# The selective scan's sum over 16 states as accumulating fp32 transposes, and projection weights held for two directions at a time

## The reference

```python
def step(h, inp):
    u_l, d_l, B_l, C_l = inp
    dA = jnp.exp(d_l[..., None] * A)
    dBu = d_l[..., None] * B_l[:, :, None, :] * u_l[..., None]
    h = dA * h + dBu
    y = jnp.sum(h * C_l[:, :, None, :], axis=-1)
    return (h, y)
```

## Time and profile before

| | us |
|---|---|
| runs of the kernel (3) | 27558.77 to 27562.47, median 27561.47 |
| span of the profiled execution | 27568.2 |
| one block of the scan in the steady part (b = 10, first sample) | 68.57 |
| the scan's stage per sample, first scan to last | 2193.7 |
| granted TensorE clock, mean over the span | 0.946 |

### The profile page before, as it was taken

The page is one execution under the profiler, slowest core; times in us unless marked ns, Lnnn a source line. Parts: engine busy times, 40 slices in busy tenths (PEclk is TensorE's granted clock), DMA queues, the critical chain, the costliest instruction groups (busy, mean ns, idle before and its releaser), DMA issues. The chain is left out here.

```text
span 27568.2 us, 304787 instructions
## 1 busy us (share of the span) xinstructions
PE 25221.1 (91%) x87136; PEld 12623.8 (46%) x87136; DVE 23267.7 (84%) x22864; ACT 21119.6 (77%) x39912; POOL 21256.1 (77%) x9545
## 2 busy tenths in 40 slices
PE   8999879998799987999879998799987999879998
PEld 3455434554345543455434554345543455434554
DVE  6799867998679986799867998679986799867998
ACT  4799747997479974799747997479974799747997
POOL 3799737997379973799737997379973799737997
PEclk8999989999899998999989999899998999989999
DMA  0122101221012210122101221012210122101221
GB/s 8 46 63 63 45 10 46 63 63 45 9 46 63 63 45 10 46 63 63 45 9 46 63 63 45 9 46 63 63 45 8 46 64 63 45 8 46 64 63 45
DMA packets 796847, 1243.41 MB, mean 45 GB/s; under 512 B 220801, under 2 KB 238081, under 8 KB 792065
## 3 DMA queue, kind: packets, MB, share of 16 engines
q1 hardware_dynamic: 795136, 1223.32, 15.1%
HBM read 1155.89 MB, written 67.11 MB: 44 GB/s over the span
## 5 line engine op out<-in xcount | busy, mean ns | idle before, releaser
L1590 PE MATMUL ps<-arena,ident 128*128 128x512 f32 x24576 | 11420.8, 596 | 2.8 <-DVE arena L1425 1.8
L1413 DVE TENSOR_TENSOR_SCAN arena<-arena,ps 128x512 f32<-128x512 f32 x7680 | 9263.5, 1264 | 102.1 <-ACT arena L1776 62.5
L1966 POOL TENSOR_TENSOR arena<-arena 128x1536 f32<-128x1536 f32 x1920 | 6631.5, 3459 | 72.8 <-ACT arena L1796 72.0
L1590 PEld LDWEIGHTS ps<-arena,ident 128*128 128x128 f32 x24576 | 4350.6, 190 | 4319.6 <-issue 4008.2
L1787 ACT ACTIVATE scaled<-arena,cols 128x384 f32<-128x384 f32 x10240 | 5807.7, 606 | 676.6 <-PE ps L1559 676.4
L1413 DVE TENSOR_TENSOR_SCAN arena<-ps,arena 128x512 f32<-128x512 f32 x4608 | 5583.2, 1264 | 74.7 <-ACT ps L1776 74.7
L1956 POOL TENSOR_TENSOR arena<-arena 128x1536 f32<-128x1536 f32 x1536 | 5306.2, 3463 | 321.9 <-DVE arena L1413 320.7
L1776 ACT ACTIVATE arena<-arena 128x512 f32<-128x512 f32 x7680 | 5240.7, 713 | 11.6 <-PE ps L1590 11.6
L1559 PEld LDWEIGHTS ps<-ident,scaled 128*128 128x128 f32 x30720 | 3524.8, 141 | 1982.0 <-issue 1113.1
L1559 PE MATMUL ps<-ident,scaled 128*128 128x128 f32 x30720 | 4182.0, 275 | 140.2 <-ACT scaled L1787 60.7
L1776 ACT ACTIVATE ps<-arena 128x512 f32<-128x512 f32 x4608 | 3125.0, 683 | 64.2 <-DVE arena L1413 25.1
(11 more groups left out here) (190 smaller groups left out, 33141.8 us busy)
## 6 DMA issues: line engine op xcount, KB each, us to landing
arena<-rows SPq DMA_DIRECT2D x3456, 256.0 KB, 3.2
spare<-rows SPq DMA_DIRECT2D x640, 256.0 KB, 3.3
arena<-x SPq DMA_DIRECT2D x16, 1536.0 KB, 13.4
x<-arena SPq DMA_DIRECT2D x16, 1536.0 KB, 10.7
arena<-x SPq DMA_DIRECT2D x64, 384.0 KB, 8.3
out<-arena SPq DMA_DIRECT2D x64, 384.0 KB, 3.0
rows<-xd SPq DMA_DIRECT2D x256, 64.0 KB, 2.6
arena<-L_conv_fc_w SPq DMA_DIRECT2D x16, 576.0 KB, 5.3
```

The costliest lines, as they stand in the source:

```text
L1413: nc.vector.tensor_tensor_scan(flip(states(b, n, t)), flip(decays), flip(adds), carry[:, k, N2 * n + t:N2 * n + t + 1], ALU.mult, ALU.add) ...
L1590: nc.tensor.matmul(m.ps[:, t, :], m.ident[:, :], states(b, n, t), start=False, stop=(n == SUMS[t][-1])).then_inc(at[Y_MM[t]], 1)
L1966: nc.gpsimd.tensor_tensor(out, out, each, ALU.mult).then_inc(at["hp_ready"], 1)
```

## The change

The 16 products of a tile are no longer added by a matmul with the identity as weights. Each is now the stationary operand of four 128 x 128 transposes that accumulate in bank t, so the bank holds the sum transposed, pixels on partitions. At the end of a block ACT copies the bank to an SBUF tile `y_turned` (`lift_y`), PE transposes that back into the same bank (`turn_y`, four transposes) and adds the old y or the skip product behind it in the same accumulation, and ACT copies the bank to y (`give_y`). `take_old` is gone; its product moved into `turn_y`. `lift_y` waits for the 16 sums and for the `turn_y` before (one `y_turned`), `turn_y` for its `lift_y`, `give_y` for its `turn_y`, and the first `add_up` of the next block for `give_y`. To make room for `y_turned`, the projection weights stand in two places instead of four; those of directions 2 and 3 are fetched by SP at blocks 8 and 16.

```diff
--- before.py
+++ after.py
@@ -1290,23 +1290,26 @@
 N4 = T // 128
 
 
+def rows_weights(xpw, a, k):
+
+    src = a["x_proj_w"][:, k, :].rearrange("(t p) c -> p t c", p=128)
+    return [(xpw[:, k % 2, :, 2 * NS * i:2 * NS * (i + 1)], src[:, :, DTR:]) for i in range(3)] + [
+        (xpw[:, k % 2, :, P:], src[:, :, 0:DTR])]
+
+
 def scan_weights(m, a):
 
     m.start(0)
-    xpw = m.take(K4, N2, P + DTR)
+    xpw = m.take(2 * N2, P + DTR).rearrange("p (k t) c -> p k t c", k=2)
     m.start(SLOTS)
     dtw = m.take(K4, D2)
     aneg = m.take(K4, N2, NS)
     dtb = m.take(K4, N2)
     dsk = m.take(K4, N2)
-    BC = 2 * NS
-    xw = a["x_proj_w"]
     loads = []
     for k in range(K4):
-        src = xw[:, k, :].rearrange("(t p) c -> p t c", p=128)
-        for i in range(3):
-            loads.append((xpw[:, k, :, BC * i:BC * (i + 1)], src[:, :, DTR:]))
-        loads.append((xpw[:, k, :, P:], src[:, :, 0:DTR]))
+        if k < 2:
+            loads += rows_weights(xpw, a, k)
         loads.append((dtw[P:P + DTR, k, :], a["dt_w"][:, k, :]))
         loads.append((aneg[:, k, :, :], a["A_logs"][k * D2:(k + 1) * D2, :].rearrange("(t p) n -> p t n", p=128)))
         loads.append((dtb[:, k, :], columns(a["dt_b"][k, :], 128)))
@@ -1314,7 +1317,7 @@
     return (xpw, dtw, aneg, dtb, dsk), loads
 
 
-def selective_scan(m, xc, y, weights, rows):
+def selective_scan(m, xc, y, weights, rows, a):
 
     nc = m.nc
     xpw, dtw, aneg, dtb, dsk = weights
@@ -1322,7 +1325,7 @@
     sp_l = m.take(T)
     sp_w = m.take(T)
     m.start(0)
-    m.take(K4, N2, P + DTR)
+    m.take(2 * N2, P + DTR)
     bbc = m.take(RB, T)
     cbc = [m.take(T) for _ in range(RC - 1)] + [m.spare]
     delta = m.take(2, N2, T)
@@ -1330,6 +1333,7 @@
     hs = m.take(HS, N2 * T)
     dbu = m.take(DB, N2 * T)
     turned = m.take(N4, D2)
+    y_turned = m.take(T)
     assert m.top <= 6 * SLOT, m.top
     scaled, xd, sp_e = m.scaled, m.xd, m.sp_e
     m.start(SLOTS)
@@ -1367,7 +1371,8 @@
     Y_MM = [f"y_mm_{t}" for t in range(N2)]
     names = ("filled", "ds_summed", "exped", "negated", "skip_out", "xd_mm", "hi_out", "xd_out", "mid_out", "sub_mm",
              "parts_out", "dl_mm", "sp_act", "sp_dve", "sp_pool", "kept", "turn_mm", "turn_out", "da_ready", "db_ready", "scanned",
-             "saved", "c_mm", "hc_ready", "hp_ready", "scaled_out", "back_mm", *B_IN, *C_IN, *Y_MM, "y_out")
+             "saved", "c_mm", "hc_ready", "hp_ready", "scaled_out", "back_mm", *B_IN, *C_IN, *Y_MM, "y_up", "y_turn", "y_back", "y_out",
+             "xpw_in")
 
     def nth(b, n, which):
 
@@ -1505,7 +1510,9 @@
                     return
                 if b and t == 0:
                     pe.wait_ge(at["turn_out"], (N4 + 1) * b)
-                ins = nc.tensor.matmul(shaped(b, m.ps[0:P + DTR, AH, :]), xpw[:, b // NT, t, :], block_of(b, xc, t),
+                if b >= 2 * NT and t == 0:
+                    pe.wait_ge(at["xpw_in"], 64 * (b // NT - 1))
+                ins = nc.tensor.matmul(shaped(b, m.ps[0:P + DTR, AH, :]), xpw[:, b // NT % 2, t, :], block_of(b, xc, t),
                                        start=(t == 0), stop=(t == N2 - 1))
                 if t == N2 - 1:
                     ins.then_inc(at["xd_mm"], 1)
@@ -1569,26 +1576,36 @@
                 nc.tensor.matmul(m.ps[:, CB, :], m.sel[:, NS + n:NS + n + 1].broadcast_to([P, 128]),
                                  parts[0:P, b % 2, :], start=True, stop=True).then_inc(at["c_mm"], 1)
 
-            def take_old(b, t):
-                if not exists(b):
-                    return
-                if b:
-                    pe.wait_ge(at["y_out"], N2 * (b - 1) + t + 1)
+            def turn_y(b, t):
+
+                if not exists(b):
+                    return
+                pe.wait_ge(at["y_up"], N2 * b + t + 1)
+                for j in range(N4):
+                    ins = nc.tensor.matmul(m.ps[:, t, j * 128:(j + 1) * 128], y_turned[:, j * 128:(j + 1) * 128], m.ident[:, :],
+                                           start=(j == 0), stop=False, is_transpose=True)
+                ins.then_inc(at["y_turn"], 1)
                 if b < NT:
                     pe.wait_ge(at["skip_out"], N2)
-                    nc.tensor.matmul(m.ps[:, t, :], skip[:, t, :], block_of(b, xc, t), start=True, stop=False)
+                    ins = nc.tensor.matmul(m.ps[:, t, :], skip[:, t, :], block_of(b, xc, t), start=False, stop=True)
                 else:
-                    nc.tensor.matmul(shaped(b, m.ps[:, t, :]), m.ident[:, :], block_of(b, y, t), start=True, stop=False)
+                    ins = nc.tensor.matmul(shaped(b, m.ps[:, t, :]), m.ident[:, :], block_of(b, y, t), start=False, stop=True)
+                ins.then_inc(at["y_back"], 1)
 
             def add_up(b, n, t):
                 if not exists(b):
                     return
+                if b and n == SUMS[t][0]:
+                    pe.wait_ge(at["y_out"], N2 * (b - 1) + t + 1)
                 if n in DVE_C:
                     pe.wait_ge(at["hc_ready"], nth(b, n, DVE_C) + 1)
                 else:
                     pe.wait_ge(at["hp_ready"], nth(b, n, POOL_C) + 1)
-                nc.tensor.matmul(m.ps[:, t, :], m.ident[:, :], states(b, n, t), start=False,
-                                 stop=(n == SUMS[t][-1])).then_inc(at[Y_MM[t]], 1)
+                for j in range(N4):
+                    ins = nc.tensor.matmul(m.ps[:, t, j * 128:(j + 1) * 128], states(b, n, t)[:, j * 128:(j + 1) * 128],
+                                           m.ident[:, :], start=(n == SUMS[t][0] and j == 0),
+                                           stop=(n == SUMS[t][-1] and j == N4 - 1), is_transpose=True)
+                ins.then_inc(at[Y_MM[t]], 1)
 
             for b in range(-1, BLOCKS + 1):
                 past, ahead = b - 1, b + 1
@@ -1608,14 +1625,14 @@
                 spread_c(b, 2)
                 turn_back(b, 2, 1)
                 turn_back(b, 2, 2)
+                turn_y(past, 0)
                 add_up(past, 13, 2)
                 add_up(past, 15, 1)
                 add_up(past, 13, 1)
                 add_up(past, 15, 2)
                 add_up(past, 14, 2)
                 turn_back(b, 4, 0)
-                take_old(b, 0)
-                take_old(b, 1)
+                turn_y(past, 1)
                 turn_back(b, 4, 1)
                 turn_back(b, 4, 2)
                 subtract(ahead)
@@ -1625,7 +1642,7 @@
                 turn_back(b, 5, 1)
                 turn_back(b, 5, 2)
                 spread_c(b, 5)
-                take_old(b, 2)
+                turn_y(past, 2)
                 delta_of(ahead, 0)
                 add_up(b, 1, 1)
                 add_up(b, 0, 2)
@@ -1795,10 +1812,18 @@
                 act.wait_ge(at["scanned"], N2 * (g + 1))
                 nc.scalar.copy(carry[:, k, N2 * n:N2 * (n + 1)], three(hs[:, g % HS, :])[:, :, last]).then_inc(at["saved"], 1)
 
+            def lift_y(b, t):
+                if not exists(b):
+                    return
+                act.wait_ge(at[Y_MM[t]], NS * (b + 1))
+                if N2 * b + t:
+                    act.wait_ge(at["y_turn"], N2 * b + t)
+                nc.scalar.copy(y_turned, m.ps[:, t, :]).then_inc(at["y_up"], 1)
+
             def give_y(b, t):
                 if not exists(b):
                     return
-                act.wait_ge(at[Y_MM[t]], NS * (b + 1))
+                act.wait_ge(at["y_back"], N2 * b + t + 1)
                 nc.scalar.copy(block_of(b, y, t), shaped(b, m.ps[:, t, :])).then_inc(at["y_out"], 1)
 
             nc.scalar.preload_act_table_set(LN_EXP)
@@ -1823,7 +1848,7 @@
                 scale(b, 2, 3)
                 high(ahead)
                 keep_rows(ahead)
-                give_y(past, 0)
+                lift_y(past, 0)
                 save(b, 1)
                 scale(b, 4, 0)
                 decay(b, 3, 0)
@@ -1831,9 +1856,10 @@
                 scale(b, 4, 2)
                 decay(b, 3, 1)
                 decay(b, 3, 2)
+                give_y(past, 0)
                 scale(b, 4, 3)
                 decay(b, 4, 0)
-                give_y(past, 1)
+                lift_y(past, 1)
                 decay(b, 4, 1)
                 decay(b, 4, 2)
                 decay(b, 5, 0)
@@ -1843,12 +1869,14 @@
                 scale(b, 5, 1)
                 scale(b, 5, 2)
                 scale(b, 5, 3)
+                give_y(past, 1)
                 save(b, 3)
+                lift_y(past, 2)
                 decay(b, 5, 2)
-                give_y(past, 2)
                 low_row(ahead)
                 scale(b, 7, 0)
                 decay(b, 6, 0)
+                give_y(past, 2)
                 save(b, 4)
                 scale(b, 7, 1)
                 softplus(ahead, 0, 0)
@@ -2054,9 +2082,18 @@
                     sp.wait_ge(at["hp_ready"], no - RC + 1)
                 sp.dma_start(cbc[no % RC], rows[b % 2, NS + n, :].partition_broadcast(128)).then_inc(at[C_IN[no % RC]], 16)
 
+            def load_weights(b):
```

(11 more changed lines are left out.)

## The result

| | before | after |
|---|---|---|
| median of the runs compared (4 and 3), us | 27560.12 | 28051.78 |
| median of all 4 runs, us | 27560.12 | 28055.59 |
| ratio, with its 95% interval | | 1.0178 (1.0164 to 1.0191) |
| span of the profiled execution, us | 27568.2 | 28050.2 |
| steady block, mean (least), us | 68.58 (68.55) | 70.36 (69.59) |

The change costs 492 us, 1.8%; forecast were 180. One of the changed kernel's four runs had a mean clock of 0.496 and took 47989.6 us; it and two more at a low clock (one of experiment 7, one of the kernel before) are left out of every comparison. Of the span's 482 us the stage of the scan holds 436, its end 41, all else 5 (the part before the first scan is 16 shorter, what follows the stages 20 longer). A steady block runs from its first scan to the first scan of the next; the mean is over blocks 1 to 29 of each sample, 232 in all.

What follows compares the result with a forecast made beforehand. DVE was taken to bound the kernel, PE a close second. Copies 125, stage ends 31 and clock 20 us on the span of 27568.2 gave 27744, or 27740 on the runs' median, 0.65% slower; range 27500 to 28150.

Steps and rivals of the forecast that it cites:

- A transpose that accumulates: In PE's sums: taken to cost 0.109 us like a plain transpose, though up to 0.43 us was possible.
- PE's relief is worth little: PE's block falls from about 66 us of work to 47, but DVE gets little from it.
- state 14's stall stays: DVE's idle time of 0.24 us before state 14 comes from DVE's own scan chain and keeps its length.
- The weights: Fetches on SP at blocks 8 and 16 cost nothing, with 33 us of cover; without cover 28 us.
- ACT's copies: Three more copies out of PSUM per block on ACT delay DVE by 0.5 us per block, 125 us in all.
- 0.27 for scan (4,1): On DVE: y's turn goes ahead of the transposes scan (4,1) needs, giving 0.27 us of new stall.
- PE will have them in time: PE's transposes of state 5 will be ready when ACT needs them, where ACT used to wait 0.60 us.
- state 8: ACT's lag of 0.55 us makes scan (8,0) start late, DVE 0.35 to 0.4 us late in all.
- The clock: PE's new pauses, two or three per block, lower its clock in some: 0.1 us per block, 20 us in all.
- The end of a stage: After DVE's last multiplication, lift, turn and copy home run mostly in series: 4 us per sample, 31 us in eight.
- The rival "the clock": Clock falls at pauses and stays low over the block's start: 1 to 2.5 us a block, 27900 to 28300; chance 0.13.
- The rule of the Trainium skill: Transposes do not count as busy, so PE runs nearly all the stage at 1.2 GHz: about 34000 us; chance 0.02.

Runs made afterwards that it cites:

- experiment 7: The changed kernel with turns, sums and ACT copies reordered, plus two zero-tile transposes ahead of every sum but a tile's first: 27714.35 us, 1.0054 to the kernel before.
- experiment 8: The kernel before with transposed sums, y not turned back, plus zero-tile transposes ahead of every sum but the first: 27536.05 us, 0.9992.
- experiment 1: The kernel before with only its projection weights in two places and fetched as in the change: 27568.79 us, 1.0002.
- Experiments 2: The kernel before with six ACT copies in the changed kernel's places, old-y products moved, sums still matmuls, y not turned: 28283.12 us, 1.0262.
- 4: The changed kernel with the next block's first two sums moved behind state 5's transposes in PE's list: 28233.41 us, 1.0244 to the kernel before.
- 6: The changed kernel with PE's turns of y and first sums, and ACT's third copy home and a decay, reordered: 27913.14 us, 1.0125 to the kernel before.
- Experiment 5: The changed kernel with two transposes of a zero tile ahead of every sum but a tile's first, 90 per block: 27930.72 us, 1.0131 to the kernel before.

## Why the prediction was right or wrong

The side, slower, was right, and the time is inside the range, but 27740 was far off: a cost of 180 us where 492 came.

- **A transpose that accumulates: right.** 32 in a row at the stage's end take 3.66 us, less the 0.16 us by which a record runs past the next start (0.60 for four that are 0.44 apart): 0.109 each. PE's busy share of a block was to be 47 to 50 us and is recorded as 54.7, as records run past the next start; the usual times from start to start add up to 47.1.
- **PE's relief is worth little, state 14's stall stays: right**, 0.15 us per block at experiment 8, the stall of 0.32 in every block shown. One reading behind it was off without harm: the 96 instructions of the sums are 44.6 of 68.57 us, nearly two thirds of the block and not half.
- **The weights: right**, experiment 1.
- **ACT's copies, 0.5 us per block: the first of the two terms that failed**, 1.04 measured. Of its parts 0.27 for scan (4,1) was 0.32. "PE will have them in time", of state 5's transposes, was wrong: ACT still waited 0.40 us for them (1613.82 above). The diff's `add_up` waits for `give_y`, whose copy stands late on ACT, and I had costed neither PE's wait nor what stands behind it, though the front part names both. From there the working lost track: the delay went to scans (5,0) and (6,2), 0.75 us, not to state 8, where I had looked. (6,2) had only 0.16 us to spare: in the kernel before its decay starts at 1686.68, the scan can follow 0.71 later, at 1687.39, and starts at 1687.55. Experiments 2 and 4 show parts of the chain, 6 and 7 that another order takes 0.65 of it back.

```profile
1686.68 0.69 ACT L1776 ACTIVATE ps<-arena 128x512 f32<-128x512 f32 x1
```

- **The clock, 0.1 us per block: the second that failed**, 0.75 measured. I had the falls (the mean granted clock of the steady blocks is 0.958, forecast 0.95 to 1.00) but priced one as a single turn 0.44 us late. The pauses are more than the two or three foreseen: a steady block has 4.7 of over 1 us, the longest 2.8, where the kernel before has none over 0.4. In the long low stretch above PE's products take about twice as long, and the delays follow each other through ACT to DVE. PE at full clock in block 9, around state 11, then at low in block 10:

```profile
1636.29 1.12 PE L1537 MATMUL ps<-xd,arena 12*128 12x512 f32 x2
1637.34 0.66 PE L1605 MATMUL ps<-ident,arena 128*128 128x128 f32 x4
1638.02 1.06 PE L1566 MATMUL ps<-ident,scaled 128*128 128x128 f32 x8
```

```profile
1703.14 1.06 PE L1566 MATMUL ps<-ident,scaled 128*128 128x128 f32 x8 [1.41 <-ACT scaled L1804]
...
1706.79 2.07 PE L1537 MATMUL ps<-xd,arena 12*128 12x512 f32 x2
1708.80 1.11 PE L1605 MATMUL ps<-ident,arena 128*128 128x128 f32 x4
1709.70 1.91 PE L1566 MATMUL ps<-ident,scaled 128*128 128x128 f32 x8
```

```profile
1706.05 3.62 DVE L1418 TENSOR_TENSOR_SCAN arena<-arena,ps 128x512 f32<-128x512 f32 x3
1710.86 2.45 DVE L1418 TENSOR_TENSOR_SCAN arena<-arena,ps 128x512 f32<-128x512 f32 x2 [1.19 <-ACT arena L1793]
```

  From the first start to the last end the three rows of one kind took 2.8 us and take 4.8 at the low clock, and scan (11,0), in the DVE rows, is 1.28 us late at one blow. The first low stretch of block 10, 33.5 to 36.9 us into it, makes scan (8,0) 0.73 late; the one of block 9, 34.8 to 38.2, makes none late. Experiment 5 takes 0.61 of the clock's 0.75 us back, and 7, against 6, nearly all of what it cost there (69.90 to 68.97, least 68.95).
- **The end of a stage, 31 us: 41**, the mechanism right. In four samples the tail is 14.8 us where it was 11.0, the 4 us forecast. In the other four it is 17.2 to 17.7 (17.6 in the first), and 10.2 us of it run at the low clock, where a transpose takes 0.218 us; that was left out of the term.
- **The rival "the clock"** has the measured time in its range, 27900 to 28300, but by luck. It asked 1 to 2.5 us a block of the clock alone, from falls at a block's start. The clock's part is 0.75, and in the steady blocks it is low only 33 to 61 us into the block.
- **The rule of the Trainium skill**, "TensorE: Matmul & The Clock Gate", Part 4, that the full clock does not engage for transposes, does not hold here. In a block of experiment 8, 414 of 445 matmul instructions are fp32 transposes and the mean clock of the steady blocks is 0.999; by the rule nearly all of it would have been at 1.2 GHz.

## What to carry to other kernels

Where a change adds a wait to an in-order queue, write down what stands behind it and by how much each of those is early; where the working stops at the waiting instruction, the cost shows up elsewhere (here 0.75 us per block on DVE, at two scans behind a wait of 0.82 on PE and the queue after it). An engine that is nearly full but does not bound gives little when it is relieved, and if it is TensorE its new pauses can cost the clock: price a fall by everything in the low stretch that another engine waits for, not by one product. Filling the pauses with products whose result is zero is a quick test of how much of a loss is the clock's.

## What was not expected of the hardware

- **A low stretch of the same length costs nothing or 0.5 us**, by where it falls. Blocks with a single one of 3.4 us at 34.6 to 38 us took 69.61 on average, as those at full clock in experiment 5 (69.62); with one at 57 to 60.5 they took 70.1. With 6.8 us at 43.4 to 50.2 they took 70.9. Where it costs nothing depends on the queue too: in experiment 5 one at 34.1 to 38.7 cost 0.34.
- **More work on TensorE made the kernel faster**: 90 transposes of zeros per block, about 10 us of PE's time, raised the mean granted clock of the steady blocks from 0.958 to 0.991.
- **How busy PE was just before did not foretell a fall.** It was busy 1.65 us of the 3.40 before the long low stretch and 2.02 of the 3.41 before that of block 9 (below), but 1.72 of 3.40 in the earlier trace rows, where the clock stayed. Which pause brings it down is left open, and so is whether an order exists that reaches the kernel before: of the complete kernels that keep the transposed sums the best, experiment 7, is 0.5% behind it.

```profile
1622.90:1626.31 3.41, 2.02 (x9) 1.10 (x10) 3.41 (x4) 3.41 (x8) 3.41 (x3) 1.00 0.15 52
```
